# Dynamic convolution: from pair 8 on, each quarter load waits until its group's stores have landed

## The chip, the cores and the metric

The kernel runs on one core of a Trainium2 chip. The metric is the device time of one execution in microseconds; lower is better.

## What is computed

The input `x` is 32 images of 64 channels and 56 x 56 pixels, float32. Each image gets its own 3 x 3 convolution, whose weights are a mixture of four sets; the mixture comes from the image itself:

```python
xn = _gn(x)                                    # 32 groups of 2 channels, mean and variance of each
pooled = xn.mean(axis=(2, 3))
a = relu(einsum('bc,kc->bk', pooled, fc1_w) + fc1_b)
att = softmax(einsum('bk,jk->bj', a, fc2_w) + fc2_b, axis=1)
agg_w = einsum('bk,koihw->boihw', att, weight) # (32, 64, 64, 3, 3)
agg_b = att @ bias
out = x + conv(xn, agg_w, stride 1, pad 1) + agg_b[:, :, None, None]
```

## The kernel before

**Tiling.** Two images make a pair, on the two halves of the 128 partitions; there are 16 pairs. Inputs and weights are each split into a high and a low float16 part (`xh`, `xl`, `wh`, `wl`), and TensorE (PE) forms high x high, low weights x high inputs, high weights x low inputs. A pair is worked on in four groups (`GROUPS`) of 7 rows from the upper half of the image (region 0) and 7 from the lower (region 1; for the last pair 8, 8, 8, 4). The result of a group lies in two PSUM banks of one of `SLOTS` = 3 slots; group n may begin when both evictions of group n - 3 are done (`slot_free`, on `s_res`).

**ScalarE (ACT)** evicts each bank into `o_sb` with a scale and an offset (`results`, line 914). The upper region uses `par`, which VectorE made. The lower region lies on the other half of the partitions and uses `crossed`, a copy of `par` with the halves changed over, which SyncE (SP) makes with two small DMAs of 0.5 KB (`cross_params`, line 303). For group 0 of a pair ScalarE waits for `par` before the upper eviction, and for `crossed` before the lower one. From pair 8 on its written-out order for pair p is: group 3 of pair p - 1; first half of `xh` of pair p + 1 (line 835), exponentials of p + 1; group 0 of p; second half of `xh`; `wh` of p + 1 (line 848); first half of `normalise` (line 802, in place in `x_sb`); group 1; second half of `normalise`; group 2.

**VectorE (DVE)** mixes the weights of a pair, forms `wl`, then both halves of `xl` (line 702), which need both halves of `normalise`. Then it aggregates the statistics of the pair after that (`group_stats`), ending with `sums` (line 543), and takes the first chunk's `bn_stats` of one more pair (line 458), for which all four quarters of that pair must have landed.

**TensorE** takes the groups in order. In the last third of group 0 of pair p, behind its nine taps, stands `image_sums(p + 1)`, a tiny product on `sums` of pair p + 1 (line 1005), from which VectorE makes the mixture.

**SyncE** issues nearly all transfers, in program order, from one queue. `x_sb` is a ring of `X_RING` = 4 buffers, and a quarter of pair p + 4 (392 KB, `load_quarter`, line 293) is asked for while the results of pair p go out. Up to pair 7 the stores of a pair go out in two lots, of groups 0 to 2 and of group 3. From pair 8 (`GROUPED`) on every group goes out by itself: the upper rows of both images as one DMA of 196 KB (line 309), then one of 98 KB for the lower rows of each image (line 312). They count up the semaphores `stored[p % 2][0]` by 16 and `stored[p % 2][1]` by 32 as they land. These are waited for by ScalarE before group 0 of pair p + 2 is written into the same buffer, and at the end of the kernel. `cross_params(p + 1)` comes right behind the stores of group 2. `transfers(p)` is the number of store lots of the pairs before p with the same parity.

A pair is written here with its group as (p, g): (9, 3) is group 3 of pair 9.

Of the kernel before, what the change touches and what calls it, by code (L numbers as in the profile page):

```python
# [82 lines left out]
def transfers(p):  # L83

    return sum(2 if q < GROUPED else GROUPS for q in range(p % 2, p, 2))
# [24 lines left out]
def dynamic_conv(nc, x, w_t, small, out):  # L110
# [7 lines left out]
    with ctx:  # L118
# [6 lines left out]
        def sem(name):  # L125
            return ctx.enter_context(nc.semaphore(name))
# [129 lines left out]
        stored = [[sem(f"stored{i}{r}") for r in range(2)] for i in range(2)]  # L256
# [14 lines left out]
        def upper_rows(p, g, groups=1):  # L271

            row, rows, at = band(p, g, 0)
            rows *= groups
            return out_d[p][:, row * W:(row + rows) * W], o_sb[p % 2][0][:, at:at + rows * W]

        def lower_rows(p, m, g, groups=1):

            row, rows, at = band(p, g, 1)
            rows *= groups  # L280
            return out_d[p][halves[m], row * W:(row + rows) * W], o_sb[p % 2][1][halves[1 - m], at:at + rows * W]
# [3 lines left out]
        @block.sync  # L285
        def _(sp):
            def load_quarter(p, n):
                if p >= X_RING:

                    for half in range(2):  # L290
                        sp.wait_ge(s_xl[half], p - X_RING + 1)
                pixels = slice(n * HALF // 2, (n + 1) * HALF // 2)
                sp.dma_start(x_sb[p % X_RING][:, pixels], x_d[p, :, pixels]).then_inc(x_in[p % X_RING][n % 2], 16)

            def quarter_landed(p, n):

                sp.wait_ge(x_in[p % X_RING][n % 2], 32 * (p // X_RING - (p % X_RING == 0)) + 16 * (n // 2 + 1))

            def cross_params(p):
                i = p % 2  # L300
                sp.wait_ge(s_par, p + 1)
                for m in range(2):
                    sp.dma_start(crossed[i][halves[1 - m], :], par[i][halves[m], :]).then_inc(s_outp[i], 16)

            def store_groups(p, g, groups=1):

                i, n = p % 2, GROUPS * p + g + groups - 1
                sp.wait_ge(s_res, 2 * n + 1)
                sp.dma_start(*upper_rows(p, g, groups)).then_inc(stored[i][0], 16)
                sp.wait_ge(s_res, 2 * n + 2)  # L310
                for m in range(2):
                    sp.dma_start(*lower_rows(p, m, g, groups)).then_inc(stored[i][1], 16)

            for n, (first, end) in enumerate(PIECES):
                pixels = slice(first * CHUNK, end * CHUNK)
                sp.dma_start(x_sb[0][:, pixels], x_d[0, :, pixels]).then_inc(x_piece[n], 16)

            for n, (piece, ks) in enumerate(zip(GATES, (slice(0, 2), slice(2, K)))):
                sp.wait_ge(x_piece[piece], 16)
                sp.dma_start(w_sb[:, ks, :], w_t[:, ks, :]).then_inc(s_weights[n], 16)  # L320
            sp.wait_ge(s_weights[0], 16)
            for n in range(4):
                load_quarter(1, n)
            cross_params(0)

            for p in range(2, X_RING):
                for n in range(4):
                    if n >= 2:
                        quarter_landed(p, n - 2)
                    else:  # L330
                        quarter_landed(p - 1, n + 2)
                    load_quarter(p, n)
            for p in range(GROUPED):

                store_groups(p, 0, SLOTS)
                cross_params(p + 1)
                load_quarter(p + X_RING, 0)
                store_groups(p, SLOTS)
                for n in range(1, 4):
                    if n >= 2:  # L340
                        quarter_landed(p + X_RING, n - 2)
                    load_quarter(p + X_RING, n)
            for p in range(GROUPED, PAIRS):

                for g in range(GROUPS if p < last_pair else GROUPS - 1):
                    store_groups(p, g)
                    if g == 2 and p < last_pair:
                        cross_params(p + 1)
                    if p + X_RING < PAIRS:
                        load_quarter(p + X_RING, g)  # L350
            i, g = last_pair % 2, GROUPS - 1
            sp.wait_ge(s_res, 2 * GROUPS * PAIRS - 1)
            sp.dma_start(*upper_rows(last_pair, g)).then_inc(stored[i][0], 16)
            sp.wait_ge(s_res_last, 1)
            sp.dma_start(*lower_rows(last_pair, 0, g)).then_inc(stored[i][1], 16)
            for i in range(2):
                for r in range(2):
                    sp.wait_ge(stored[i][r], 16 * (1 + r) * transfers(PAIRS + i))
# [68 lines left out]
        def _(dve):  # L427
# [340 lines left out]
            for p in range(EARLY, PAIRS):  # L768
# [14 lines left out]
                if p + 1 < PAIRS:  # L783
# [5 lines left out]
            dve.wait_ge(s_outp[i], 32 * (last_pair // 2 + 1))  # L789
            dve.wait_ge(s_conv, 2 * n + 2)  # L790
            _, rows, at = band(last_pair, GROUPS - 1, 1)
            nc.vector.tensor_scalar(o_sb[i][1][:, at:HALF], acc[n % SLOTS][1][:, 0:rows * W], crossed[i][:, 0:1],  # L792
                                    crossed[i][:, 1:2], ALU.mult, ALU.add).then_inc(s_res_last, 1)

        @block.scalar
        def _(act):
# [101 lines left out]
            def results(p, g, regions=range(2)):  # L898
                i, n = p % 2, GROUPS * p + g
                for r in regions:  # L900
                    if g == 0:
                        if r == 0:
                            act.wait_ge(s_par, p + 1)
                        else:
                            act.wait_ge(s_outp[i], 32 * (p // 2 + 1))
                        if p == 0:
                            act.wait_ge(s_wsquares, 1)
                            act.wait_ge(s_moments, 2)
                        if p >= 2:
                            act.wait_ge(stored[i][r], 16 * (1 + r) * transfers(p))  # L910
                    act.wait_ge(s_conv, 2 * n + r + 1)
                    scales = (par, crossed)[r][i]
                    _, rows, at = band(p, g, r)
                    nc.scalar.activation(o_sb[i][r][:, at:at + rows * W], acc[n % SLOTS][r][:, 0:rows * W], ACT.Identity,  # L914
                                         bias=scales[:, 1:2], scale=scales[:, 0:1]).then_inc(s_res, 1)
# [318 lines left out]
```

## Time and profile before

| | |
|---|---|
| median of 3 runs | 304.8 us (304.75 to 305.0) |
| the profiled execution | 304.24 us |
| its span, first to last instruction | 302.5 us |
| TensorE busy | 297.2 us, 98% of the span |
| weight loads busy | 273.1 us, 90% |
| VectorE busy | 245.9 us, 81% |
| ScalarE busy | 189.7 us, 63% |
| GpSimd busy | 17.7 us, 6% |
| granted clock of TensorE | 1.0 in the whole span |
| DMA | 53.62 MB, mean 177 GB/s |

The profile is of one execution. Its time is 0.56 us under the median; 1.7 us of it lie outside the span. Busy times of the engines overlap, so an engine's idle time costs something only if it is on the chain that ends last. DMA-issuing instructions are not counted as busy; in a timeline they stand as `SPq`, with the time that the issue took, and "to landing" is the time from the start of the issue to the last semaphore event of that transfer.

### The profile page before, as it was taken

Reading aid. Unit: us, or ns where it says so; the run is one execution under the profiler, and the core shown is the slowest. Engines: PE = TensorE matmul, PEld = TensorE weight load, DVE = VectorE, ACT = ScalarE, POOL = GpSimd, SP = SyncE. Lnnn points to the kernel's source line nnn. Section 1 sums busy time; section 2 is a strip of 40 time slices with the busy share of each in tenths; the row PEclk is TensorE's granted clock in tenths of the full one; section 3 lists DMA queues with packets and bytes.
Section 4 is the critical chain, followed back from the end, with each engine's and each line's share of the span. In section 5 each row is a group of like instructions: output and inputs, shape, how many; then the busy total and the mean of one; then the engine's idle time right before and its main releaser. Section 6 shows DMA issues by size and latency. Waiting matters only on the chain.

```text
span 302.5 us, 15876 instructions
## 1 busy us (share of the span) xinstructions
PE 297.2 (98%) x7065; PEld 273.1 (90%) x7065; DVE 245.9 (81%) x799; ACT 189.7 (63%) x246; POOL 17.7 (6%) x30
## 2 busy tenths in 40 slices
PE   8999999999999999999999999999999999999995
PEld 6778997799978997799999999999999999999874
DVE  4898989989999999898998989699696978956000
ACT  3757739194674927385496868577585866768222
POOL 2231040403100000000000000000000000000000
PEclk9999999999999999999999999999999999999999
DMA  7857866647457583846708788765657242332333
GB/s 268 317 168 214 262 184 200 215 146 191 152 163 218 175 243 135 223 144 173 258 14 245 239 242 266 204 197 165 191 150 240 95 123 70 111 102 81 93 113 104
DMA packets 27012, 53.62 MB, mean 177 GB/s; under 512 B 6080, under 2 KB 16704, under 8 KB 26944
## 3 DMA queue, kind: packets, MB, share of 16 engines
q1 hardware_dynamic: 26720, 52.53, 57.6%
q8 instruction: 55, 0.90, 1.2%
q14 instruction: 13, 0.11, 0.1%
q10 hardware_dynamic: 224, 0.07, 0.1%
HBM read 26.89 MB, written 25.69 MB: 174 GB/s over the span
## 4 chain that ended last, share of the span: by engine, by line
PE 95%; DMA 3%; ACT 0%; POOL 0%; DVE 0%; issue 0%; DVEq 0%
PE acc L1068 94%; DMA w_sb<-w_t 1%; DMA x<-x 1%; ACT o L875 0%; PE acc L1048 0%; PE acc L1036 0%; PE tiny L1005 0%; POOL wnorms L418 0%; DVE o L792 0%; PE tiny L1022 0%; PE tiny L1026 0%; PE acc L1042 0%; DVEq L790 0%
## 5 line engine op out<-in xcount | busy, mean ns | idle before, releaser
L1068 PE MATMUL acc<-xh,wh 64*64 64x385 f16 (+5 forms) x2304 | 112.6, 325 | 0.0
L1068 PE MATMUL acc<-xh,wl 64*64 64x385 f16 (+5 forms) x2304 | 112.4, 325 | 0.0
L1068 PE MATMUL acc<-xl,wh 64*64 64x385 f16 (+5 forms) x2304 | 111.7, 325 | 0.0
L1068 PEld LDWEIGHTS acc<-xl,wh 64*64 64x64 f16 x2304 | 91.3, 107 | 6.0
L1068 PEld LDWEIGHTS acc<-xh,wl 64*64 64x64 f16 x2304 | 90.6, 107 | 6.8
L1068 PEld LDWEIGHTS acc<-xh,wh 64*64 64x64 f16 x2304 | 89.5, 107 | 7.2 <-ACT wh L864 0.3
L914 ACT ACTIVATE o<-acc,par 128x392 f32<-128x392 f32 (+1 forms) x64 | 42.9, 671 | 56.9 <-PE acc L1068 56.9
L458 DVE BATCH_NORM_STATS2 stats<-x 128x6 f32<-128x448 f32 x105 | 61.2, 617 | 1.8
L835 ACT ACTIVATE xh<-x,xof,xsc 128x1568 f16<-128x1568 f32 x24 | 40.5, 1689 | 25.1 <-DVE xof L545 24.6
L702 DVE TENSOR_TENSOR xl<-x,xh 128x1568 f16<-128x1568 f32 x28 | 49.8, 1783 | 3.3 <-ACT x L802 3.2
L593 DVE SCALAR_TENSOR_TENSOR mix<-w_sb,ex,mix 128x576 f32<-128x576 f32 (+1 forms) x69 | 42.8, 620 | 0.5
L914 ACT ACTIVATE o<-acc,crossed 128x392 f32<-128x392 f32 (+1 forms) x63 | 42.4, 672 | 0.2 <-DMA crossed<-par 0.2
L802 ACT ACTIVATE x<-x,xof,xsc 128x1568 f32<-128x1568 f32 x20 | 33.7, 1685 | 0.0
L792 DVE TENSOR_SCALAR o<-acc,crossed 128x224 f32<-128x224 f32 x1 | 0.5, 509 | 19.4 <-PE acc L1068 19.4
L395 POOL TENSOR_TENSOR xl<-x,xh 128x840 f16<-128x840 f32 (+1 forms) x8 | 13.3, 1678 | 51.0 <-DVE xl L702 51.0
L553 DVE SCALAR_TENSOR_TENSOR prod<-tiny,small_sb 128x20 f32<-128x20 f32 x16 | 2.8, 177 | 15.9 <-PE tiny L1005 15.6
L848 ACT ACTIVATE wh<-mix,wsc 128x576 f16<-128x576 f32 (+2 forms) x13 | 9.5, 737 | 7.9 <-DVE mix L600 7.9
L693 DVE SCALAR_TENSOR_TENSOR wl<-mix,wsc,wh 128x576 f16<-128x576 f32 x15 | 12.1, 805 | 1.1 <-ACT wh L848 1.1
L896 ACT ACTIVATE ex<-logit,nmax 128x4 f32<-128x4 f32 x16 | 4.7, 293 | 11.7 <-DVE nmax L557 11.4
L1048 PE MATMUL acc<-ones 128*128 128x256 f16 x69 | 10.0, 312 | 1.4 <-POOL eye L373 1.4
L591 DVE TENSOR_SCALAR mix<-w_sb,ex 128x576 f32<-128x576 f32 (+1 forms) x22 | 9.2, 420 | 2.5 <-ACT ex L896 2.4
L1048 PEld LDWEIGHTS acc<-ones 128*128 128x128 f16 x69 | 7.5, 115 | 3.3 <-POOL eye L373 1.3
(106 smaller groups left out, 161.6 us busy)
## 6 DMA issues: line engine op xcount, KB each, us to landing
x<-x SPq DMA_DIRECT2D x60, 392.0 KB, 4.0
out<-o SPq DMA_DIRECT2D x36, 196.0 KB, 3.6
out<-o SPq DMA_DIRECT2D x72, 98.0 KB, 2.8
out<-o SPq DMA_DIRECT2D x8, 588.0 KB, 3.3
out<-o SPq DMA_DIRECT2D x16, 294.0 KB, 4.2
w_sb<-w_t SPq DMA_DIRECT2D x2, 576.0 KB, 4.1
x<-x SPq DMA_DIRECT2D x2, 448.0 KB, 4.2
out<-o SPq DMA_DIRECT2D x7, 112.0 KB, 2.2
```

The source lines that it names most:

```text
L395: nc.gpsimd.tensor_tensor(xl[i][:, start:end], x_sb[p][:, start:end], xh[i][:, start:end], ALU.subtract).then_inc(done, 1)
L458: ins = nc.vector.bn_stats(stats[:, 0, 6 * t:6 * t + 6], x_sb[p % X_RING][:, t * CHUNK:(t + 1) * CHUNK])
L591: ins = nc.vector.tensor_scalar(**columns, scalar1=ex[:, 0:1], scalar2=None, op0=ALU.mult)
L593: ins = nc.vector.scalar_tensor_tensor(**columns, scalar=ex[:, k:k + 1], in1=mix[:, part], op0=ALU.mult, op1=ALU.add)
L693: nc.vector.scalar_tensor_tensor(out=wl[i][:], in0=mix[:], scalar=wsc[i][:], in1=wh[i][:], op0=ALU.mult, op1=ALU.subtract).then_inc(s_wl, 1)
L702: nc.vector.tensor_tensor(rows_of(xl[i], half), rows_of(x_sb[p % X_RING], half), rows_of(xh[i], half), ALU.subtract).then_inc(s_xl[half], 1)
L802: nc.scalar.activation(v, v, ACT.Identity, bias=xof[i][:], scale=xsc[i][:]).then_inc(s_xn[half], 1)
L835: nc.scalar.activation(rows_of(xh[i], half), rows_of(x_sb[p % X_RING], half), ACT.Identity, bias=xof[i][:], scale=xsc[i][:]).then_inc(s_xh ...
L848: nc.scalar.activation(high[:, rows], mixed_w[:, rows], ACT.Copy, scale=wsc[i][:]).then_inc(s_wh, 1)
L914: nc.scalar.activation(o_sb[i][r][:, at:at + rows * W], acc[n % SLOTS][r][:, 0:rows * W], ACT.Identity, bias=scales[:, 1:2], scale=scales[ ...
L1048: nc.tensor.matmul(acc[SLOTS - 1][0][:, 0:2 * P], ones[:].bitcast(fp16)[:, 0:P], ones[:].bitcast(fp16), start=True, stop=True)
L1068: ins = nc.tensor.matmul(pixels[:, top:bottom, left:right], weights[i][halves[m], tap * C:(tap + 1) * C], window, start=start and step == ...
```

## The change

In the loop of SyncE over pairs 8 to 15, where a quarter of pair p + 4 is asked for (pairs 8 to 11, four groups each), SyncE first waits until the stores that it has just issued for this group have landed, upper and lower. The counts are exact: 16 for each earlier upper lot of the same parity and one for this group, 32 for the lower ones. `cross_params(p + 1)`, behind the stores of group 2, stands ahead of that wait. There are 16 places with two waits each, in all 32 wait instructions; nothing is removed.

```diff
@@ -347,6 +347,9 @@
                     if g == 2 and p < last_pair:
                         cross_params(p + 1)
                     if p + X_RING < PAIRS:
+
+                        for r in range(2):
+                            sp.wait_ge(stored[p % 2][r], 16 * (1 + r) * (transfers(p) + g + 1))
                         load_quarter(p + X_RING, g)
```

## Rows read from the trace of the kernel before

**Rows 1.** The page, busy us of each engine, share of the span, instructions.
```profile
...
PE 297.2 (98%) x7065; PEld 273.1 (90%) x7065; DVE 245.9 (81%) x799; ACT 189.7 (63%) x246; POOL 17.7 (6%) x30
...
```

**Rows 2.** Windows of one pair: length, PE, PEld, DVE, ACT, POOL busy, clock, DMA.
```profile
...
192.26:210.08 17.82, 17.82 (x444) 17.68 (x440) 14.88 (x50) 12.17 (x15) 0.00 (x0) 1.00 0.62 175
...
245.72:263.54 17.82, 17.82 (x444) 17.68 (x440) 14.87 (x50) 12.17 (x15) 0.00 (x0) 1.00 0.35 99
...
```

**Rows 3.** Waits: who waited for whom, us in all, times, longest.
```profile
...
ACT o L914 <- DMA crossed<-par: 0.2, 1, 0.2
...
```

**Rows 4.** Timeline of SP, pairs 8 and 11: start, us, line, operation.
```profile
...
170.00 0.95 SPq L309 DMA_DIRECT2D out<-o  x1
...
172.20 0.53 SPq L293 DMA_DIRECT2D x<-x  x1
172.78 0.44 SPq L309 DMA_DIRECT2D out<-o  x1
...
225.21 0.35 SPq L309 DMA_DIRECT2D out<-o  x1
225.78 1.12 SPq L312 DMA_DIRECT2D out<-o  x2
226.94 1.24 SPq L303 DMA_DIRECT2D crossed<-par  x2
...
```

**Rows 5.** Lower stores (L312) of 169.9 to 232, issue ns, us to landing.
```profile
...
L312 SPq DMA_DIRECT2D out<-o x32: 466/592/2155, 171.0 to 230.8; - x32
...
DMA to landing us min/median/max: 2.1/3.4/4.8
```

**Rows 6.** The same of 232.1 to 290, where no loads are issued.
```profile
...
L312 SPq DMA_DIRECT2D out<-o x26: 466/597/1783, 234.6 to 288.4; - x26
...
DMA to landing us min/median/max: 2.1/2.2/4.1
```

**Rows 7.** Timeline of ScalarE, pair 9, and the lower eviction (12, 0).
```profile
...
180.75 0.68 ACT L914 ACTIVATE o<-acc,crossed 128x392 f32<-128x392 f32 x1 [0.23 <-DMA crossed<-par]
181.33 1.68 ACT L835 ACTIVATE xh<-x,xof,xsc 128x1568 f16<-128x1568 f32 x1
183.90 0.78 ACT L848 ACTIVATE wh<-mix,wsc 128x576 f16<-128x576 f32 x1 [0.89 <-DVE mix L600]
184.59 1.68 ACT L802 ACTIVATE x<-x,xof,xsc 128x1568 f32<-128x1568 f32 x1
186.17 0.66 ACT L914 ACTIVATE o<-acc,par 128x392 f32<-128x392 f32 x1
...
187.30 1.69 ACT L802 ACTIVATE x<-x,xof,xsc 128x1568 f32<-128x1568 f32 x1
...
233.89 0.67 ACT L914 ACTIVATE o<-acc,crossed 128x392 f32<-128x392 f32 x1
...
```

**Rows 8.** Timeline of VectorE, pair 10's low inputs and pair 11's statistics.
```profile
...
187.22 3.59 DVE L702 TENSOR_TENSOR xl<-x,xh 128x1568 f16<-128x1568 f32 x2
...
193.23 0.15 DVE L543 TENSOR_TENSOR sums<-std,wbound 128x1 f32<-128x1 f32 x1
...
193.70 0.63 DVE L458 BATCH_NORM_STATS2 stats<-x 128x6 f32<-128x448 f32 x1
...
```

**Rows 9.** Timeline of TensorE: group 3 of pair 12 begins; sums of pair 14.
```profile
...
241.01 0.33 PE L1068 MATMUL acc<-xh,wh 64*64 64x392 f16 x2
...
249.99 0.23 PE L1005 MATMUL tiny<-sums,ones 64*64 64x6 f32 x4
...
```

**Rows 10.** The two lower stores of pair 8, group 0.
```profile
...
L312 SPq DMA_DIRECT2D out<-o x2: 472/534/596, 171.0 to 171.5; - x2
...
DMA to landing us min/median/max: 2.7/2.8/2.8
```

**Rows 11.** All `crossed` transfers (L303) of 169.9 to 284.
```profile
...
DMA to landing us min/median/max: 1.8/2.6/3.6
```

**Rows 12.** Quarter loads (L293) of 169.9 to 232.
```profile
...
DMA to landing us min/median/max: 3.1/4.2/5.3
```

## The prediction, made before the changed kernel was run

> **What bounds the kernel now.** I read the page first. TensorE is busy for 297.2 of 302.5 us [rows 1], and the chain that ended last is its products. Next I read the stretches from one group-3 eviction to the same one a pair later. From pair 9 on each pair takes 17.82 us, TensorE is busy for all of it, and that is the same with a DMA share of 0.62 and of 0.35 [rows 2]. So in this stage TensorE waits for nothing: work that moves on the sync engine (SP) can't make it faster, only make something late for it. The question is how much lateness there is room for. The one place where ScalarE already waits for a transfer shows where to look: 0.2 us for `crossed` [rows 3], just before the lower half of pair 9's group 0 is evicted.
>
> **What is queued behind the new waits.** SP issues everything in order: the stores of a group, `cross_params` of the next pair, the quarter load. Today a store is issued and SP goes on at once; in pair 8 it is a little behind already, since the stores of group 0 at 170.00, the load at 172.20 and the next stores at 172.78 follow one another without a gap [rows 4]. With the change SP stands still after each group of pairs 8 to 11 until all three stores have landed: 16 stops. Three things are behind them.
>
> First, the load itself. Second, the stores of later groups; nobody needs their buffer before the pair after next. Third, `cross_params(p+1)`, which is issued between the stores of group 2 and the wait, so it stands behind the stops of all groups before it. ScalarE waits for it before the lower eviction of group 0 of pair p+1, and behind that eviction stand on ScalarE the second half of `xh`, `wh`, both halves of `normalise` and the evictions of groups 1 and 2.
>
> **One cycle of SP.** While SP is behind, the period between the stores of one group and those of the next is c = load issue + from the upper store's start to the last lower store's start + landing of that last one + resuming. The load's issue takes 0.58 (172.20 to 172.78). From the upper store to the second lower one it is 225.78 - 225.21 + half of 1.12 = about 1.1 [rows 4]; slow issues occur (0.95 against some 0.4 for the upper store at 170.00), and I take 1.2. Resuming: 0.06, an estimate from the gaps of 0.05 to 0.1 us between these rows. The landing is the unknown. With loads around, a lower store lands after 3.4 at the median and 4.8 at most [rows 5]; in the stage without loads after 2.2 at the median and 4.1 at most [rows 6]. The changed order lies between: the queue is empty when the load is issued, but the 392 KB load stands directly ahead of the 392 KB of stores, and nothing comes behind them until they have landed. I take 3.0, a little over the middle of the two medians, because the *last* of three must land and the slow ones count. So c = 0.58 + 1.2 + 3.0 + 0.06 = 4.84 us. The bounds are c = 4.0 (landing 2.2) and c = 5.3 (3.4); 6.7 if each took the longest.
>
> The Trainium skill's page "DMA: Bandwidth & Descriptors" (section "Anatomy of one DMA — SWDGE (gpsimd) path") prices one transfer, on another issue path than this, at some 2.0 us plus its bytes over 436 GB/s: 2.23 us for a lower store of 100,352 bytes, which the median of [rows 6] agrees with. For a load and its three stores as one stream (802,816 bytes) that would be 3.84 us from the load's issue, so a cycle of 3.9 and no loss at all; it speaks against my term, and the medians with loads around are what speaks for it.
>
> **What the cycle has to beat.** Four cycles per pair against TensorE's 17.82: SP keeps up only if c is under 4.455. With 4.84 it takes 19.36 per pair and falls 1.54 us further behind with each.
>
> **When lateness reaches TensorE.** From the landing of `crossed` (T) the chain is, with the distances between starts where an engine runs on: lower eviction 0.58 (180.75 to 181.33), `xh` 1.60 (1.69 less the overlap), `wh` 0.69 (183.90 to 184.59), first `normalise` 1.58 (to 186.17), two evictions 1.13 (to 187.30), second `normalise` 1.69 [rows 7]; then VectorE's second half of `xl`, half of 3.59 = 1.79, and from its end at 190.81 to the end of `sums` at 193.38, 2.57 [rows 8]. Together 11.63, and 0.1 until TensorE uses it: T + 11.7. TensorE is in order, and `image_sums` (the `tiny` product) stands in its queue at the end of group 0 of the following pair: at 249.99 for the cross of pair 12 [rows 9]. So that cross may land as late as 238.3, 4.4 us later than ScalarE uses it now (233.89). A nearer use is the bank: group 3 of pair 12 starts at 241.01 [rows 9] and needs the evictions of group 0, T + 0.7; that binds later than the other does, so it costs nothing on top. The mix of the next pair's weights is ready before ScalarE comes to `wh` (it waits 0.9 us for it now, and will not when it is late).
>
> **The sum.** Stores of pair 8, group 0, are unchanged: the last one starts at 171.5 and lands 2.8 later at most [rows 10], 174.3. Load, then stores of (8,1) at 175.0. The crosses' second issue starts 2.3 after the upper store (226.94 + 0.6 - 225.21) and lands 2.6 later [rows 4, 11], 4.9 in all. So the cross of pair 9 lands at 175.0 + c + 4.9 = 184.7; its limit is three periods before 238.3, 184.8. Not late by itself, but all the room is used. From there each pair adds 1.54:
>
> - cross of pair 10: 204.1 against 202.7, 1.4 late
> - cross of pair 11: 223.5 against 220.5, 3.0 late
> - cross of pair 12: 242.8 against 238.3, 4.5 late
>
> Pair 11 is the last with waits. Behind it SP issues a group's stores in some 1.8 us again; group 2 of pair 12 is evicted at about T + 8.4 = 251.2, so the cross of pair 13 lands at about 256, before its limit of 238.3 + 17.8 + 4.5 = 260.6. TensorE has nothing to make the loss up with, and the last stores are as before. Loss = 13c - 58.4: 4.5 us; zero at c = 4.49; 1.3 us more for each 0.1 us of cycle. Against the profiled execution (304.24, of which 302.5 is the span) that is 308.7; the median of the runs is 0.56 higher, so 309.3 us. The 32 waits themselves cost only SP.
>
> **The loads.** The last quarter of pair 12 is asked for at 175.0 + 3c - 0.6 = 188.9 and lands at most 5.3 later [rows 12], 194.2. VectorE reads it today at 193.70 [rows 8], but in the changed kernel not before T + 11.63 + 0.3, 196.6. Pair 15: asked for at 247.0, landed by 252.3, read after 254.7. Hidden, with 2.4 us to spare.
>
> **Rivals.**
>
> *SP keeps up* (0.17). If the stores land within 2.65 us behind a load on an otherwise empty queue, c is at most 4.49, each store is out when the next group comes, and nothing changes: 304.8. For it: 26 lower stores in a quiet queue have a median of 2.2 [rows 6]. Against: even there some take up to 4.1, one slow one in four cycles adds half a microsecond per cycle, and here a load of the same size is ahead. This is the case on the other side, not slower; it decides at c = 4.49. The page of the Trainium skill named above, in the same section, would have it so.
>
> *The landing stays as it is among loads* (0.20). If a load directly ahead is what makes the 3.4 and more of [rows 5], c is 5.3 or over: 13 x 5.3 - 58.4 = 10.5, so 315.3; at c = 5.5 it would be 317.9. Against: many of those stores share the queue with the next load, which the change holds back.
>
> *The loads become the wait* (0.03). VectorE would stop at `bn_stats` of the next pair. It takes loads that land over 7.7 us after issue; none took over 5.3. Each 1 us beyond would be 1 us of TensorE: some 311.
>
> *No effect, since the wait is satisfied when reached*: excluded, the counts include the stores just issued, and a lower store lands after 2.1 us at the least [rows 6].
>
> *Faster* (0.03). A quieter queue could land `crossed` earlier, but only 0.2 us is waited for there [rows 3] and TensorE doesn't see it. I know of no mechanism.
>
> **Chances and range.** My forecast (c from 4.5 to 5.3, 304.9 to 315.3): 0.57; SP keeps up 0.17; c over 5.3 0.20; loads 0.03; faster 0.03. A measurement of this kernel can tell about 0.2%, 0.6 us, from no change: faster 0.03, within 0.17, slower 0.80. The range takes in the case of no change and ends where c is 5.4: 304.6 to 316.
>
> **What would show it.** SP's waits: a new one for `out<-o` of some 2 to 3.5 us, 16 times. Stores of pairs 8 to 11 4.8 us apart with no wait for ScalarE between them. ScalarE's wait for `crossed`, 0.2 us in total before, longer with each pair from 9 to 12 and gone from 13 on. TensorE idle before `tiny` and at the first low products of pairs 10 to 13, pair periods of 19.4 there and 17.82 behind. Wrong if: the waits are under 2 us and SP still waits for ScalarE (SP keeps up), or the pair periods grow with `crossed` in time (then something else that I don't see).

## The result: 318.67 us, 4.6% slower, and the profile after

The changed kernel takes 318.67 us (median of 4, 317.91 to 319.86) against 304.77 us for the kernel before: a ratio of 1.0462, interval 1.0444 to 1.048, a loss of 13.9 us. The profiled execution took 319.86 us, its span is 318.0. The direction was as forecast and the measured time lies outside the range of 304.6 to 316. Medians here and below are of the runs within 1.5% of a kernel's fastest; one run of the longer pause, 328.18 us, lies outside and is left out.

The page of the changed kernel, busy shares and the chain that ended last, by engine and by line:

```profile
PE 300.8 (95%) x7065; PEld 261.9 (82%) x7065; DVE 246.4 (77%) x799; ACT 188.4 (59%) x246; POOL 17.7 (6%) x30
...
PE 67%; DMA 16%; SPq 6%; ACT 6%; issue 2%; DVE 1%; POOL 0%; ACTq 0%; DVEq 0%
PE acc L1071 66%; DMA out<-o 9%; DMA crossed<-par 5%; SPq L312 3%; ACT x L805 2%; SPq L309 2%; ACT xh L838 2%; DMA w_sb<-w_t 1%; ACT o L917 1%; DMA x<-x 1%; SPq L293 1%; SPq L303 1%; ACT wh L851 1%; ACT o L878 0%; PE acc L1039 0%
```

Against [rows 1] TensorE's share of the span fell from 98 to 95%. Before the change 95% of the chain was TensorE's; now it leaves TensorE for a third of the time, and the largest part of that is the landing of stores, followed by `crossed`. Waits of the changed kernel (us in total, times, longest):

```profile
ACT o L917 <- DMA crossed<-par: 29.9, 4, 10.1
...
PE acc L1071 <- ACT o L917: 8.4, 5, 4.2
...
PE tiny L1008 <- DVE sums L546: 2.3, 4, 0.8
```

and those of SyncE:

```profile
SPq L309 <- ACT o L917: 67.9, 22, 9.0
SPq L291 <- DMA out<-o: 43.9, 16, 4.5
```

ScalarE's wait for `crossed` was 0.2 us, once [rows 3]; now it is 29.9 in four pairs. VectorE has no new wait for `x`: the loads, though late, were hidden. SyncE's 16 waits for `out` are the new stops, 43.9 us in all. They are 2.7 us on the mean because a stop begins only when the issues before it are through. The chain in order of time (start, length, what), from 195 us on, shows the loop that now sets the pace:

```profile
195.29 0.33 SPq L293
195.67 0.43 SPq L309
196.14 1.73 SPq L312
197.92 2.58 DMA out<-o
200.56 0.33 SPq L293
200.94 0.43 SPq L309
201.41 0.47 SPq L312
201.93 0.60 SPq L312
202.57 0.59 SPq L303
203.21 4.40 DMA crossed<-par
207.63 0.69 ACT o L917
...
```

Load, upper store, two lower stores, landing, next load: SyncE is the bottleneck, and at 207.63 ScalarE gets its `crossed`. The four late lower evictions, with what ended the idle time before each, from the timeline of ScalarE:

```profile
185.93 0.68 ACT L917 ACTIVATE o<-acc,crossed 128x392 f32<-128x392 f32 x1 [4.93 <-DMA crossed<-par]
...
207.63 0.68 ACT L917 ACTIVATE o<-acc,crossed 128x392 f32<-128x392 f32 x1 [7.41 <-DMA crossed<-par]
...
232.02 0.68 ACT L917 ACTIVATE o<-acc,crossed 128x392 f32<-128x392 f32 x1 [10.10 <-DMA crossed<-par]
...
253.81 0.68 ACT L917 ACTIVATE o<-acc,crossed 128x392 f32<-128x392 f32 x1 [7.50 <-DMA crossed<-par]
```

and the sums on TensorE at the end of group 0 of pairs 9 to 14, which answer to [rows 9]:

```profile
179.19 0.23 PE L1008 MATMUL tiny<-sums,ones 64*64 64x6 f32 x4
...
197.61 0.22 PE L1008 MATMUL tiny<-sums,ones 64*64 64x6 f32 x2 [0.43 <-DVE sums L546]
...
219.31 0.23 PE L1008 MATMUL tiny<-sums,ones 64*64 64x6 f32 x2 [0.79 <-DVE sums L546]
...
243.70 0.23 PE L1008 MATMUL tiny<-sums,ones 64*64 64x6 f32 x2 [0.32 <-DVE sums L546]
...
265.49 0.22 PE L1008 MATMUL tiny<-sums,ones 64*64 64x6 f32 x2 [0.79 <-DVE sums L546]
...
283.36 0.23 PE L1008 MATMUL tiny<-sums,ones 64*64 64x6 f32 x4
```

The distances are 18.42, 21.70, 24.39, 21.79 and 17.87 us, against 17.82 in every pair before [rows 2]. The excess is 15.1 us, which is the growth of the span (15.5) but for 0.4. And from the start of the late eviction to the sums it is 11.68 us each time (197.61 - 185.93 and so on): the chain that the prediction put together as 11.7.

### The profile page after: what moved, and what is told of

It reads as the page before. It is cut to its first block, busy times and chain, and to the rows that moved or that the text cites. A ratio compares the mean times of both kernels' runs of the same rounds, so it can differ in the third digit from the quotient of the medians.

```text
span 318.0 us, 15892 instructions
## 1 busy us (share of the span) xinstructions
PE 300.8 (95%) x7065; PEld 261.9 (82%) x7065; DVE 246.4 (77%) x799; ACT 188.4 (59%) x246; POOL 17.7 (6%) x30
## 4 chain that ended last, share of the span: by engine, by line
PE 67%; DMA 16%; SPq 6%; ACT 6%; issue 2%; DVE 1%; POOL 0%; ACTq 0%; DVEq 0%
PE acc L1071 66%; DMA out<-o 9%; DMA crossed<-par 5%; SPq L312 3%; ACT x L805 2%; SPq L309 2%; ACT xh L838 2%; DMA w_sb<-w_t 1%; ACT o L917 1%; DMA x<-x 1%; SPq L293 1%; SPq L303 1%; ACT wh L851 1%; ACT o L878 0%; PE acc L1039 0%
## 5 line engine op out<-in xcount | busy, mean ns | idle before, releaser
L1071 PE MATMUL acc<-xh,wh 64*64 64x385 f16 (+5 forms) x2304 | 110.8, 327 | 8.4 <-ACT o L917 8.4
L1071 PE MATMUL acc<-xh,wl 64*64 64x385 f16 (+5 forms) x2304 | 110.5, 327 | 0.0
L1071 PE MATMUL acc<-xl,wh 64*64 64x385 f16 (+5 forms) x2304 | 109.1, 325 | 0.5 <-DVE xl L705 0.5
L1071 PEld LDWEIGHTS acc<-xh,wh 64*64 64x64 f16 x2304 | 85.5, 108 | 21.0 <-ACT o L917 8.5
L1071 PEld LDWEIGHTS acc<-xh,wl 64*64 64x64 f16 x2304 | 87.2, 108 | 11.0
L1071 PEld LDWEIGHTS acc<-xl,wh 64*64 64x64 f16 x2304 | 87.2, 107 | 10.5 <-issue 1.2
L917 ACT ACTIVATE o<-acc,crossed 128x392 f32<-128x392 f32 (+1 forms) x63 | 42.4, 673 | 29.9 <-DMA crossed<-par 29.9
L823 ACT ACTIVATE xh<-x,xof,xsc 128x784 f16<-128x784 f32 x9 | 9.3, 1032 | 0.0
L812 ACT ACTIVATE x<-x,xof,xsc 128x784 f32<-128x784 f32 x9 | 8.9, 1026 | 0.0
```

The lines of the kernel that those rows point to most:

```text
L1071: ins = nc.tensor.matmul(pixels[:, top:bottom, left:right], weights[i][halves[m], tap * C:(tap + 1) * C], window, start=start and step == ...
```

## The experiments

Theory A is that of the prediction: what costs is `crossed`, queued on SyncE behind the stops. Its number is the cycle c, the mean distance between the upper stores of successive groups from (8, 1) to (11, 2), and a loss of 13c - 58.4. The other letters are rivals, and each is defined in the expectation where it first stands. All runs were timed beside the kernel before on the same chip (its medians: 304.68 to 304.77). Each c comes from the one execution that was profiled.

**Loads on an idle engine.** The load and its delay move to GpSimd:

```diff
-                    if p + X_RING < PAIRS:
-                        for r in range(2): sp.wait_ge(stored[p % 2][r], ...)
-                        load_quarter(p + X_RING, g)
# GpSimd, at its end, for p in 8..11 and n in 0..3
+                    pool.wait_ge(s_res, 2 * (GROUPS * p + n + 2))
+                    pool.wait_ge(s_xl[0], p + 1); pool.wait_ge(s_xl[1], p + 1)
+                    pool.dma_start(x_sb[...], x_d[p + X_RING, ...]).then_inc(x_pool[...], 16)
```

> The quarter loads of pairs 12 to 15 are issued by GpSimd, which is idle, and each still waits: until the next group has been evicted, some 3 to 6 us. SyncE has no stop and no load in pairs 8 to 11. Theory A (what costs is what stands on SyncE behind the stops, crossed above all): loss under 0.6 us, 304.8 us, no wait for crossed over 0.3 us. Rival B (the loads come late and VectorE stops at the statistics): they are still asked for late, so a good part of the 13.9 us stays, over 309 us. Rival C (issuing loads apart from stores is itself bad for TensorE, for instance by its clock or by memory traffic): over 309 us too, with no wait named.

Measured: 304.47 us, ratio 0.9997 (0.9988 to 1.0007). ScalarE still waited 4.2 us for `crossed`, in two places and at most 2.4, so the "no wait over 0.3" was wrong; TensorE had the room for it. Loads asked for some us later, by an engine with nothing behind the wait, cost nothing. B and C fall; for the changed kernel itself, B falls also by its waits, where VectorE has none for these loads.

**`crossed` out of the way, stops kept.**

```diff
-                    if g == 2 and p < last_pair:
+                    if g == 0 and p < last_pair:
                         cross_params(p + 1)
```

> As the changed kernel, but cross_params of the next pair is issued behind the stores of group 0, two cycles earlier. Theory A: ScalarE's wait for crossed, 29.9 us in all, falls to under 8 us. By crossed alone the loss would be 11c - 58.4 = 3.6 us with the measured cycle of 5.64. But SyncE is as late as ever with the loads: the last quarter of pair 15 would land at about 260 to 263 against 247.15, with some 6 us of room, so VectorE now waits for loads and the loss is 7 to 10 us, 312 to 315 us. Rival B (loads were the cause all along): 318 to 319 us as with the change. If neither crossed nor loads matter: 318 too.

Measured: 308.93 us, 1.0137 (1.0103 to 1.0171), a loss of 4.2 us where the change loses 13.9. Waits of this kernel:

```profile
DVE stats L461 <- DMA x<-x: 15.6, 4, 6.4
...
ACT o L917 <- DMA crossed<-par: 0.2, 1, 0.2
```

With `crossed` ahead, its wait is what it was before the change, and the second thing in SyncE's queue comes up: VectorE waits for loads. The last quarter of pair 15 was asked for at 252.81; in the kernel before, VectorE had read that pair at 247.15. I had expected 7 to 10 us, 312 to 315. The cycle was 5.23 instead of 5.64, and 15 cycles of 0.41 less make the last load 6 us earlier.

**Stops without a load.** The wait moves out of the `if`, to all pairs up to 14:

```diff
+                    if p < last_pair:
+                        for r in range(2): sp.wait_ge(stored[p % 2][r], ...)
                     if p + X_RING < PAIRS:
-                        for r in range(2): sp.wait_ge(stored[p % 2][r], ...)
                         load_quarter(p + X_RING, g)
```

> As the changed kernel, and SyncE also stops behind the groups of pairs 12 to 14, where no load follows. It measures the cycle without a load ahead. If the load ahead in the queue makes the landing long, the cycle here is 3.6 to 4.2 us when SyncE is behind, under TensorE's 4.455, SyncE catches up, and the time is that of the changed kernel within 1 us: 318 to 320. If stores land late whatever is ahead of them (cycle 5.2 or more), crossed of pairs 13 to 15 falls behind too and the time is 325 us or more.

Measured: 319.89 us, 1.0506 (1.0479 to 1.0533), 15.1 us. Timeline of SyncE from (12, 1) to (13, 1):

```profile
265.38 0.35 SPq L309 DMA_DIRECT2D out<-o  x1
...
268.55 0.34 SPq L309 DMA_DIRECT2D out<-o  x1
...
272.08 0.34 SPq L309 DMA_DIRECT2D out<-o  x1
...
276.32 0.34 SPq L309 DMA_DIRECT2D out<-o  x1
...
279.50 0.34 SPq L309 DMA_DIRECT2D out<-o  x1
```

Four cycles in 14.12 us: 3.5 each, under TensorE's 4.455, and SyncE catches up. The 12 further stops add 1.2 us, no more than the spread of either kernel's runs (317.91 to 319.86 and 319.21 to 321.12), so it isn't the stop that costs, but a stop whose cycle is longer than TensorE's group.

**Fewer pairs with stops.**

```diff
-                        for r in range(2):
+                        for r in range(2 if p < GROUPED + 2 else 0):
```

> As the changed kernel, but the stops are only in pairs 8 and 9; pairs 10 and 11 ask for their loads as before. Theory A: the last crossed behind stops is that of pair 10, and the loss is 5c + 179.9 - 202.7 = 5.4 us at c = 5.64 (4.0 to 7.0 for c from 5.35 to 5.95): 310.2 us. A loss in proportion to the stops, as for a price per wait: half of 13.9, 311.7. Rival B: loads of pairs 12 and 13 are late, those of 14 and 15 are not: the time depends on them alone, no forecast better than 305 to 312, but with VectorE waiting for x.

Measured: 308.46 us, 1.0125 (1.0105 to 1.0145), 3.7 us: half the stops, a quarter of the loss. That is under the 4.0 to 7.0 us expected, since c was smaller than assumed, and far from the 7 us of a price per wait. The upper stores of (8, 1) and (9, 2) left at 175.72 and 201.54, c = 5.16; the line with the measured start gives 201.54 + 4.9 - 202.7 = 3.7.

**Load ahead of the stop.**

```diff
+                        load_quarter(p + X_RING, g)
                         for r in range(2):
                             sp.wait_ge(stored[p % 2][r], 16 * (1 + r) * (transfers(p) + g + 1))
-                        load_quarter(p + X_RING, g)
```

> The same 16 stops, but the load is issued ahead of the stop instead of behind it: stores, (crossed,) load, wait for the stores, next stores. The load has then some 3 us of head start on the next stores instead of 0.4. Theory A with the load directly ahead as what makes the stores land late (they landed in 3.5 us cycles where no load was ahead, in 5.6 us with one): cycle 3.9 to 4.5, SyncE keeps up, loss 0 to 1.5 us, 304.8 to 306.3 us. Rival D (the load behind the stores slows them as much as one ahead): the last lower store lands some 4.5 us after its issue, cycle 5.5 or more, loss 13c - 58.4 of 13 us or more, 318. Rival E (a price per stop): 318.7 too.

Measured: 305.6 us, 1.0037 (1.0014 to 1.006), 0.9 us. The ten runs spread from 304.32 to 307.39, wider than those of the kernel before. The profiled one took 306.86. From (8, 1) at 175.27 to (11, 2) at 232.82 its c is 4.43. Over the first five cycles, however, it is 4.89, above the 3.9 to 4.5 expected, so that the cross of pair 10 was some 2 us late, close to the 2.2 us that this execution lost. ScalarE waited 14.2 us for `crossed` in four pairs, most of it inside TensorE's room. D and E fall.

**Stop for the upper store alone.**

```diff
-                        for r in range(2):
+                        for r in range(1):
```

> As the changed kernel, but each stop waits only for the upper store, not for the two lower ones. The upper store is issued 1.1 us ahead of the last lower one and landed 3.6 to 5.8 us after its issue, so the cycle becomes 0.38 + 4.3 + 0.06 = 4.7 to 4.9. Theory A by the line of the cycle, loss = 13c - 58.4: 2.7 to 5.3 us, 307.5 to 310 us. A price per stop or per load delayed would leave most of the 13.9 us.

Measured: 309.5 us, 1.0182 (1.0132 to 1.0231), 4.8 us. c = (237.15 - 174.82)/13 = 4.79, as expected, and the line gives 3.9. Here the cross of pair 11 is the one that is latest: its upper store left at 220.00, and 220.00 + 4.9 - 220.5 = 4.4.

**Both moves, all 16 stops.** `crossed` behind group 0 and the load ahead of the stop.

> The same 16 stops with both moves: crossed behind the stores of group 0, and the load issued ahead of the stop. Neither crossed nor the loads are then behind. Theory A: no wait for crossed, no wait of VectorE for x, 304.8 us within 0.6 (304.2 to 305.4). Anything that a stop costs by itself, whatever is queued behind it, would remain: over 306 us.

Measured: 304.58 us, 0.9995 (0.9979 to 1.0011), with this among SyncE's waits, none of ScalarE for `crossed` and none of VectorE for the late loads:

```profile
SPq L308 <- DMA out<-o: 22.4, 14, 3.1
```

SyncE stands still for 22.4 us and the kernel is as fast as the one before. It does not beat it, and nothing here did: there is no idle TensorE to win back.

**Half a load.** This kernel leaves out half of each late load, and its outputs are wrong by that; only its time is of use.

```diff
-                pixels = slice(n * HALF // 2, (n + 1) * HALF // 2)
+                width = HALF // 4 if p >= GROUPED + X_RING else HALF // 2
+                pixels = slice(n * HALF // 2, n * HALF // 2 + width)
```

> As the changed kernel, but the loads of pairs 12 to 15 bring only the first half of each quarter, 196 KB instead of 392, so that work of the loads is left out and the outputs of those pairs come from old pixels in the other halves. It changes one size: what is directly ahead of the stores. The cycle was 3.5 us with nothing ahead and 5.6 us with 392 KB. If the length of the load is what counts: 4.5 to 4.6, loss by 13c - 58.4 of 0 to 1.5 us, 304.8 to 306.3 us. If it is any load ahead, whatever its size: cycle 5.2 or more, loss over 9 us, over 314 us.

Measured: 314.13 us, 1.0311 (1.0253 to 1.0369), 9.4 us. c = (243.43 - 175.95)/13 = 5.19. Nothing ahead 3.5, half a load 5.2, a whole one 5.6. The forecast by size, 4.5 to 4.6 and 304.8 to 306.3 us, falls. These are means over cycles of two kinds, which "Open" below takes apart.

**Pauses.** In the changed kernel's own trace the last lower store lands in two ways. The two lower stores of (10, 0) and then of (11, 1):

```profile
L312 SPq DMA_DIRECT2D out<-o x2: 472/540/607, 214.4 to 214.9; - x2
...
DMA to landing us min/median/max: 3.4/4.0/4.5
```

```profile
L312 SPq DMA_DIRECT2D out<-o x2: 473/535/597, 245.0 to 245.5; - x2
...
DMA to landing us min/median/max: 2.2/2.3/2.3
```

The first was issued 1.4 us behind its load (213.52), the second 2.4 (243.10), since a slow issue of the upper store, 1.47 us, lay between. I took that for a cause and put satisfied waits in three places:

```diff
+            def pause():
+                for _ in range(20): sp.wait_ge(s_weights[0], 16)   # 50 in the last of the four
...
# first kernel: behind load_quarter; second: ahead of the last lower store; third: ahead of load_quarter
```

> As the changed kernel, with 20 waits that are long satisfied behind each of the 16 loads: a pause of some 1 us between a load and the next stores. In the changed kernel's trace the last lower store lands after 4.3 to 5.3 us when it is issued within 1.5 us of the load, and after 2.2 to 2.6 where a slow issue put it 2.1 us or more behind the load. Theory F (four transfers issued close together delay the last of them by some 2 us): every last lower store lands in under 3 us, the cycle stays at 4.7 to 5.0 in spite of the pause, and the loss falls to 3 to 7 us, 308 to 312 us: a pause makes it faster. Rival G (slow issue and quick landing have only a common cause; the landing doesn't hang on the distance): the pause comes on top, cycle 6.4 to 6.7, loss 24 us or more, over 328 us.

Measured: 318.04 us, 1.0439 (1.0417 to 1.046); c = (246.50 - 175.46)/13 = 5.46. The pause was 0.6 us.

> As the changed kernel, with the same pause of some 1 us ahead of the last lower store of each group in pairs 8 to 11, so that load, upper and first lower store stay close together. Theory F: it lands in under 3 us too, cycle 4.7 to 5.1, 308 to 313 us. If the distance of the upper store from the load is what counts (the load must be through first), the last store lands late still: cycle 6 or more, over 323 us.

Measured: 319.43 us, 1.0482 (1.0446 to 1.0517), c = 5.58.

> The control: the same pause, but behind the stop and ahead of the load, where load and stores stay close together. The cycle is longer by the pause, 6.4 to 6.8 with the landing as it was. By 13c - 58.4 the loss is 25 to 30 us, 330 to 335 us. If a pause anywhere quickens the landing: under 320 us.

Measured: 318.75 us, 1.0456 (1.0432 to 1.048), c = 5.43. It is no control: only 0.1 us lies between landing and load, so this pause didn't take place as meant.

The forecasts of F and G both fail. The three cycles are 0.06 to 0.21 us under the 5.64 of the changed kernel, which itself is one execution: no effect of the pause can be told from that. A longer one:

> As e10, with 50 satisfied waits instead of 20 behind each load; 20 took 0.6 us, so some 1.55 us. With 0.6 us the last store was issued later by as much and landed 5.7 to 6.2 us behind the load's issue as before. If the end is set from the load (something still runs until 5.9 us behind it), the cycle stays at 5.7 to 6.1 here too and the time at 317 to 320 us, the pause costing nothing. If the distance of 2.1 us counts after all, as in the cycles with a slow issue, all last stores land in 2.2 to 2.6: cycle 5.3 to 5.6, 314 to 318 us. If the pause comes on top: cycle 6.6, 328 us.

Measured: 322.79 us, 1.0588 (1.052 to 1.0656); the profiled execution took 324.74. c = (254.60 - 177.30)/13 = 5.95, inside the 5.7 to 6.1 of the first reading (the end of a cycle is set from the load), though the time is over its 317 to 320. The pause of 1.5 us costs 0.3 per cycle: most of it lay beside something that is under way anyhow. Not all last stores landed quickly, they took 2.2 to 4.0 us, so the second reading falls; the third, 6.6 us, falls too.

**The load in another queue.** As the first experiment, but SyncE keeps its stops:

```diff
# on top of the loads on GpSimd
+                    if p + X_RING < PAIRS:
+                        for r in range(2): sp.wait_ge(stored[p % 2][r], ...)
```

> SyncE keeps its 16 stops, as in the changed kernel, but the loads are issued by GpSimd (as in e1, one group later, through a queue of its own), so no load is ahead of the stores in SyncE's queue, while the same bytes pass through the same DMA engines at about the same time. If the load must be directly ahead in the same queue to delay the last store: cycle 3.5 to 4.2, SyncE keeps up, under 0.8 us of loss, 304.0 to 305.6 us. If a load on the same DMA engines is enough: the last lower store lands after 4 us and more where a load runs beside it, cycle 4.6 to 5.6 while SyncE is behind, loss of 2 us or more, over 306.7 us.

Measured: 309.33 us, 1.016 (1.012 to 1.0199), 4.6 us. c = (238.61 - 176.80)/13 = 4.75. Timelines of SyncE and of GpSimd:

```profile
182.26 0.34 SPq L310 DMA_DIRECT2D out<-o  x1
...
185.44 0.34 SPq L310 DMA_DIRECT2D out<-o  x1
...
191.09 0.34 SPq L310 DMA_DIRECT2D out<-o  x1
...
196.64 0.34 SPq L310 DMA_DIRECT2D out<-o  x1
```

```profile
187.19 0.54 POOL L433 DMA_DIRECT2D x<-x  x1 [9.76 <-ACT o L927]
192.15 0.54 POOL L433 DMA_DIRECT2D x<-x  x1 [4.43 <-ACT o L927]
194.87 0.54 POOL L433 DMA_DIRECT2D x<-x  x1 [2.18 <-ACT o L927]
```

From 182.26 to 185.44, with no load under way, a cycle is 3.2 us. The next two, with a load of GpSimd beside them, are 5.65 and 5.55. So a load need not be ahead of the stores in their queue for c to stay over TensorE's 4.455. How much of the difference is the load's is not shown: in both long cycles a packet of the instruction queue (see "Open" below) started among the issues too, and the two lower stores took 2.10 and 2.34 us to issue, against 1.11.

The Trainium skill ("DMA: Bandwidth & Descriptors", section "Queues, rings and completion order") says that a completion's increment lands only after every earlier write of the same DMA engine, across its queues. No run here shows that rule at work. In the first long cycle the last store was issued at 186.3 and the load only at 187.19.

## Why the prediction was right in direction and wrong in size

**What held.** TensorE had nothing to gain, SyncE's stops put `crossed` behind (the runs with the loads on GpSimd, with `crossed` ahead and with both moves show it by taking one or the other away), and the loads were hidden in the changed kernel. The chain of 11.7 us was 11.68 four times. The line from cycle to loss held over the runs that keep all 16 stops and in which `crossed` was the limit:

| run | c, us | (11, 2) leaves | its cross late, us | measured loss, us |
|---|---|---|---|---|
| the change | 5.64 | 248.15 | 14.8 | 13.9 |
| load halved | 5.19 | 243.43 | 10.0 | 9.4 |
| pause behind the load | 5.46 | 246.50 | 13.1 | 13.3 |
| pause ahead of the last store | 5.58 | 249.25 | 15.9 | 14.7 |
| pause ahead of the load | 5.43 | 246.19 | 12.8 | 14.0 |
| longer pause | 5.95 | 254.60 | 21.2 | 18.1 |
| loads on GpSimd, stops kept | 4.75 | 238.61 | 5.2 | 4.6 |
| upper store only | 4.79 | 237.15 | 3.8 | 4.8 |

The fourth column is the third + 4.9 - 238.3, the prediction's limit. The losses are medians; the cycles come from one execution each. The two columns agree within 1.2 us but for the longer pause, whose profiled execution lost 20.0.

**The step that failed** is the term "landing of that last one", 3.0 us, in the sum c = 4.84. Measured in the changed kernel, the 15 last stores of (8, 1) to (11, 3) landed after 2.2 to 5.3 us, 3.9 on the mean. The rest of the sum was off by little: 1.33 instead of 1.2 from the upper to the last store, 0.38 instead of 0.58 for the load (an issue out of a stop took 0.33), 0.06 for resuming. 0.38 + 1.33 + 3.9 + 0.06 = 5.67, against the measured 5.64. Each 0.1 us of cycle is 1.3 us of time, so 0.8 us too little became 10 us: 4.5 forecast, 14.9 by the line with the true cycle.

Two things went into the 3.0. I read a median over both lower stores [rows 5], where only the later of the two counts. And I took the quiet queue as half of the truth, because nothing would be behind the stores. But c was 5.64 with a load ahead and 3.5 in the four cycles without one. Of these 2.1 us the load's own issue is 0.38, and the landing most of the rest: 3.9 on the mean against 2.5. The prediction's rival "the landing stays as it is among loads", with 0.20, is what happened: it gave 315.3 at c = 5.3 and 317.9 at 5.5. Its case was priced, but the range left it out, since I had bounded c by a median (3.4) and not by the slow landings. (The range's end of 316 is c = 5.35 by the line; c = 5.4 gives 316.6.)

"SP keeps up" did not happen. Of the signs, 16 waits for `out` came, 2.7 us on the mean. The stores were 5.6 us apart and not 4.8. The excess of a pair was 0.6, 3.9, 6.6 and 4.0 us instead of an even 1.54, because the cycles were uneven. The formula of the Trainium skill's page "DMA: Bandwidth & Descriptors" (section "Anatomy of one DMA — SWDGE (gpsimd) path"), which is given there for another issue path, did not hold for the stream: 3.84 us for a load and its stores, against 5.64 for the cycle. For a lone lower store its 2.23 us agrees with the 2.2 of the quick ones.

**Open, and what the traces say of it.** The last store landed now in 2.2 to 2.6 us and now in 4.3 to 5.3 behind the same load, and once in 3.3. Neither size nor distance explains it alone. One thing in the trace goes with it: a single packet of 0.02 MB on the queue that the profile calls `q8 instruction`, some 0.9 us of one engine (an estimate: 1.0% of 16 engines over 5.87 us). The cycle from 219.45 to 225.32 has one:

```profile
q1 hardware_dynamic: 448, 0.80, 47.2%
q8 instruction: 1, 0.02, 1.0%
```

and that from 231.71 to 236.47 is the only one of the fifteen without:

```profile
GB/s 0 0 0 0 0 0 0 0 237 211 79 132 132 79 79 79 132 211 184 184 290 409 382 422 395 395 356 395 395 369 330 277 277 172 119 27 0 0 0 0
...
q1 hardware_dynamic: 448, 0.80, 61.6%
issues: line engine op xcount, KB each, median us to landing
```

The 15 cycles of the changed kernel, by the time from the load's issue to the start of that packet (read from windows of 0.25 us and less):

| packet starts | cycles | upper store to last store, us | last store lands, us | whole cycle, us |
|---|---|---|---|---|
| 0.5 to 1.0 us behind the load | 5 | 1.7 to 2.3 | 2.2 to 2.6 | 4.7 to 5.3 |
| 1.25 | 1 | 1.0, its own issue 1.9 | 4.3 | 5.7 |
| 2.9 to 4.1 | 8 | 1.0 | 4.4 to 5.3 | 5.9 to 6.8 |
| none | 1 | 1.0 | 3.3 | 4.76 |

So a packet that falls into SyncE's issues goes with a slow issue, and one that falls behind them with a late landing. The run with stops in all pairs has the same classes, with 4.70 us and a landing of 3.3 for its cycle without a packet. In the run with `crossed` ahead the packet started within 1.2 us of the load in all 16 cycles, which goes with its smaller c.

Cycles in which no such packet started before the last store had landed took 3.17 and 3.18 us with no load (stops in all pairs), 3.93 with half a load (one cycle) and 4.76 and 4.70 with a whole one: there a load costs 1.55 us and half a load half of it, so its size does count, on the few cycles there are. With the load followed by a pause of 0.6 and of 1.5 us they were 4.82 and 5.12. The prediction's 4.84 was nearly right for such a cycle. What its landing term had at nothing is the packet, which 14 of 15 cycles contain. This is read from the traces. No run moved or removed the packets, so that they are the cause is not shown.

How a late packet could delay a landing is shown no better. The moved bytes of one slow cycle, (10, 0), in 40 slices from 213.5 to 219.5:

```profile
DMA  0000009999147559999999998831000000000000
GB/s 0 0 0 0 0 0 105 209 146 105 42 63 146 146 209 397 376 376 366 454 366 366 397 389 293 282 105 31 10 10 21 31 21 21 21 10 0 0 0 0
```

Nearly everything has moved by the 27th slice, 4 us from the start; in the nine slices after that 10 to 31 GB/s trickle, where the cycle without the packet ends in no such tail. One of 16 engines would move some 25 at the rate of the busy slices (397), so an estimate is that a single engine is late. The trace does not tell on which engine a packet ran.

## What to carry to other kernels

A wait on a queue's engine costs by what stands behind it in that queue: list those items with the room of each, and compare the queue's cycle with the period of the bottleneck engine. Below the period a stop is free (with both moves 22 us of standing still, no loss), above it the excess adds up with every cycle. Where a group of transfers must land, take the landing of the last of them, beside the traffic that will be there, the program's own instruction packets included. Compare single cycles before explaining their mean. And carry the slope of the loss into the range: here it multiplied an error of 0.8 us by 13.

## What was not expected

TensorE's granted clock fell after its longest wait for ScalarE. TensorE stood for 4.17 us until 232.75, and in the stretches from 231.7 on (length, busy us of PE, PEld, DVE, ACT, POOL, clock, DMA share, GB/s) it was:

```profile
231.70:232.70 1.00, 0.00 (x0) 0.00 (x0) 0.00 (x0) 0.68 (x2) 0.00 (x0) 1.00 0.11 19
232.70:235.30 2.60, 2.55 (x40) 1.66 (x44) 0.32 (x1) 2.60 (x3) 0.00 (x0) 0.62 0.94 248
235.30:238.00 2.70, 2.70 (x56) 1.82 (x52) 2.70 (x4) 2.70 (x4) 0.00 (x0) 0.74 0.41 85
```

A mean of 0.62 and 0.74 means that part of each stretch ran at 1.2 instead of 2.4 GHz. It cost nothing on top, since the sums of that pair came 11.68 us behind its eviction like all others: TensorE, slower, was still waiting for ScalarE and VectorE.
